# Cached attention: four score units in a row, then one whole value product; a VectorE read-out moved ahead of a transpose

## What is computed

```python
L = NPP * PSIZE                                   # 16 pages x 32 keys
kc = k_cache[block_table].reshape(bsz, L, HK, D)
k_all = jnp.concatenate([kc, k], axis=1)          # 512 cached keys + 32 own = 544
scores = jnp.einsum('bqhd,bkhd->bhqk', q, k_all) * SCALE
scores = jnp.where(valid[:, None, None, :], scores, -1e+30)
probs = jax.nn.softmax(scores, axis=-1)
o = jnp.einsum('bhqk,bkhd->bqhd', probs, v_all)
```

## Time and profile before

| | before |
|---|---|
| median of three runs | 3048.9 us |
| lowest, highest run | 3042.11, 3051.08 us |
| span of the profiled execution | 3042.6 us |
| TensorE matmul busy | 3015.9 us (99%) |
| VectorE busy | 1866.3 us (61%) |
| ScalarE busy | 1541.9 us (51%) |
| GpSimd busy | 609.8 us (20%) |

### The profile page before, as it was taken

One profiled execution on the slowest core, in us unless ns is written; L12 is line 12 of the kernel. 1 busy time (PEld: TensorE's weight loads), 2 busy tenths in 40 slices (PEclk: granted clock), 3 DMA queues, 4 the chain that ended last, 5 costly groups with the idle time before them and its releaser, 6 DMA issues.

```text
span 3042.6 us, 91714 instructions
## 1 busy us (share of the span) xinstructions
PE 3015.9 (99%) x36256; PEld 2345.8 (77%) x36256; DVE 1866.3 (61%) x3587; ACT 1541.9 (51%) x2949; POOL 609.8 (20%) x1462
## 2 busy tenths in 40 slices
PE   8999999899999999999999999999999999999999
PEld 7777778667777777777777888888888888888887
DVE  5777779487888888788786444432333333544544
ACT  6666655377777777777776222212333334322221
POOL 0000001354554554554551000000000000300000
PEclk9999999999999999999999999999999999999999
DMA  5333335566766666666667434413333333843311
GB/s 163 110 104 111 110 111 154 177 211 213 217 206 209 216 211 207 214 212 211 214 213 226 124 110 124 118 77 107 97 94 104 119 103 88 242 149 111 110 42 56
DMA packets 506613, 456.02 MB, mean 150 GB/s; under 512 B 33985, under 2 KB 470593, under 8 KB 501698
## 3 DMA queue, kind: packets, MB, share of 16 engines
q1 hardware_dynamic: 470402, 354.41, 38.4%
q0 software_dynamic: 35904, 96.85, 9.6%
HBM read 321.03 MB, written 130.02 MB: 148 GB/s over the span
## 4 chain that ended last, share of the span: by engine, by line
PE 79%; DMA 1%; DVE 0%; issue 0%; ACT 0%; DVEq 0%; SPq 0%
PE ps_o L1009 18%; PE ps_scores L993 16%; PE s_ps L58 8%; PE s_ps L60 8%; PE s_ps L59 8%; PE s_ps_proj L58 5%; PE s_ps_proj L59 5%; PE s_ps_proj L60 5%; PE s_ps_o L1542 1%; PE s_ps_scores L1518 1%; PE yv_ps L59 1%; PE yv_ps L60 1%; PE yv_ps L58 1%; PE s_ps L1717 0%; PE s_ps L1708 0%
## 5 line engine op out<-in xcount | busy, mean ns | idle before, releaser
L1009 PEld LDWEIGHTS ps_o<-weights_t,v_all 32*128 32x128 f32 x17408 | 510.2, 187 | 108.7 <-issue 108.6
L1009 PE MATMUL ps_o<-weights_t,v_all 32*128 32x128 f32 x17408 | 559.2, 276 | 4.1 <-issue 2.3
L993 PE MATMUL ps_scores<-k_slot,q_slot 128*32 128x288 f32 (+1 forms) x8192 | 525.7, 397 | 6.7 <-PEq L98 4.8
L898 ACT ACTIVATE probs<-masked,shift 128x544 f32<-128x544 f32 x512 | 382.9, 748 | 246.2 <-DVE shift L944 244.2
L944 DVE CUSTOM_DVE_ANT_0 masked<-ps_scores,reach,scale_now 128x544 f32<-128x544 f32 x512 | 390.1, 762 | 173.1 <-PE ps_scores L993 169.4
L993 PEld LDWEIGHTS ps_scores<-k_slot,q_slot 128*32 128x32 f32 x8192 | 242.1, 110 | 199.7 <-issue 8.6
L957 DVE STREAM_TRANSPOSE weights_t<-probs 128x544 f32<-128x544 f32 x512 | 376.8, 736 | 23.8 <-ACT probs L903 10.1
L903 ACT ACTIVATE probs<-probs,inv 128x544 f32<-128x544 f32 x512 | 375.7, 734 | 0.0
L1101 ACT ACTIVATE s_h_hi<-s_h_raw 128x2048 fp32r<-128x2048 f32 x64 | 122.8, 1919 | 487.4 <-PE s_ps L60 481.1
L84 POOL COPY k_slot<-k_pool 128x256 f32 x1024 | 358.9, 409 | 20.7 <-issue 20.1
L58 PE MATMUL s_ps_proj<-y_hi,s_w_hi 128*128 128x512 f32 x640 | 253.3, 396 | 0.0
(11 more groups left out here) (202 smaller groups left out, 4733.4 us busy)
## 6 DMA issues: line engine op xcount, KB each, us to landing
v_all<-vpool_in SPq DMA_DIRECT2D x1024, 128.0 KB, 3.0
qT_scratch<-k_pool SPq DMA_DIRECT2D x32, 1024.0 KB, 5.1
q_slot<-qT_scratch POOLq DMA_DIRECT2D x64, 512.0 KB, 3.5
oT_scratch<-o_t POOLq DMA_DIRECT2D x128, 256.0 KB, 4.9
s_h_raw<-oT_scratch SPq DMA_DIRECT2D x32, 1024.0 KB, 5.7
aT_scratch<-s_o_t SPq DMA_DIRECT2D x32, 1024.0 KB, 5.6
s_h_raw<-aT_scratch SPq DMA_DIRECT2D x32, 1024.0 KB, 5.7
w_raw<-w_in SPq DMA_DIRECT2D x11, 1024.0 KB, 7.7
```

The source lines that it names most:

```text
L898: act.activation(probs[:, k % BUF, :], masked[:, k % 2, :], ACT.Exp, bias=shift[:, k % BUF:k % BUF + 1], scale=-1.0, accum_out=total[:, k ...
L993: m = pe.matmul(ps_scores[q * S:(q + 1) * S, k % 2, cols], q_slots[j][:, head, r * S:(r + 1) * S], k_slots[j][:, pages, head * PSIZE:(head ...
L1009: m = pe.matmul(ps_o[:, q, 0:GS], v_all[rows, j, t, e * D:(e + 1) * D], weights_t[rows, g, :, t * S:(t + 1) * S], start=t == 0, stop=t == NPP)
```

## The change

TensorE now takes four units of scores in a row and then all 17 blocks of one group's values. On VectorE the second unit's `lowest` in each group is issued before the transpose that it used to follow; `inverse` stays between the two `lowest`. `reach_of` moves from the third unit of a batch to its fifth (`k % HK == G`), the first of its second group.

```diff
             def pair_of(i, first, last):
                 for k in range(2 * HK):
                     n, g = i * 2 * HK + k, k // G
-                    if k % HK == 2 and not (last and k > HK):
+                    if k % HK == G and not (last and k > HK):
                         reach_of(i * 2 + k // HK + 1, 1 - k // HK)
-                    lowest(n, k, i * 2 + k // HK)
+                    if k % G != 1:
+                        lowest(n, k, i * 2 + k // HK)
                     if not (first and k == 0):
                         inverse(n - 1, k - 1)
+                    if k % G == 0:
+                        lowest(n + 1, k + 1, i * 2 + k // HK)
                     if not (first and k < 2):
                         turn(n - 2, (k - 2) % (2 * HK), i * 4 + (k - 2) // G)
...
-            parts = (range(0, SPLIT), range(SPLIT, NPP + 1))
-
-            def pair_of(i, first):
-                for k in range(0, 2 * HK, 2):
-                    n, g = i * 2 * HK + k, k // G
-                    for d in range(2):
-                        scores(n + d, k + d, i * 2 + k // HK)
-                    if not (first and g < 2):
-                        values(i * 4 + g - 2, (g - 2) % 4, i if g >= 2 else i - 1, parts[k // 2 % 2])
...
+            for grp in range(GROUPS):
+                for n in range(grp * G, grp * G + G):
+                    scores(n, n % (2 * HK), n // HK)
+                if grp >= 2:
+                    values(grp - 2)
+            for grp in (GROUPS - 2, GROUPS - 1):
+                values(grp)
```

More of the change, by code:

```diff
@@ L987, in scores @@
                     pe.wait_ge(k_gathered, b + 1)
-                if not isinstance(n, int) or n >= 2:
+                if n >= 2:
                     pe.wait_ge(shift_done, n - 1)
@@ L995, in scores, with values @@
                 m.then_inc(scores_done, 1)
[L997 to L1006, removed]
+            def values(grp):
+                b, e, g = grp // 2, grp % 2, grp % 4
+                j = b % 2
+                if e == 0:
+                    pe.wait_ge(v_loaded[j], b // 2 * 16 * NPP + 16 * NPP)
+                    pe.wait_ge(v_own_loaded[j], b // 2 * 16 + 16)
+                pe.wait_ge(turned_w, grp * G + G)
+                pe.wait_ge(o_copied, grp + 1)
+                for t in range(NPP + 1):
                     for q in range(SEQ):
@@ L1010, in values @@
                                       weights_t[rows, g, :, t * S:(t + 1) * S], start=t == 0, stop=t == NPP)
-                if pages[-1] == NPP:
-                    m.then_inc(pv_done, 1)
-            parts = (range(0, SPLIT), range(SPLIT, NPP + 1))
-            def pair_of(i, first):
-                for k in range(0, 2 * HK, 2):
-                    n, g = i * 2 * HK + k, k // G
-                    for d in range(2):
-                        scores(n + d, k + d, i * 2 + k // HK)
-                    if not (first and g < 2):
-                        values(i * 4 + g - 2, (g - 2) % 4, i if g >= 2 else i - 1, parts[k // 2 % 2])
[L1024 to L1028, removed]
+                m.then_inc(pv_done, 1)
+            for grp in range(GROUPS):
[5 more added lines that the diff above has]
+                values(grp)
     return dict(sync=sync, gpsimd=gpsimd, scalar=scalar, vector=vector, tensor=tensor,
```

## The result

The changed kernel takes 3057.85 us (median of five runs, 3055.61 to 3060.11) against 3042.45 us before in the same rounds. The ratio on record is 1.0037, 95% interval 1.0025 to 1.0049: 0.37% slower, 11.3 us on 3042.45, with 7.6 to 14.9 inside the interval. It isn't the quotient of the two medians: these lie 15.4 us apart and the means 12.2, because the five runs before fall apart into three at 3042 and two at 3049 and 3051 us. The forecast was +10.3 us, 1.0034 times before.

What follows compares the result with a forecast made beforehand. TensorE was taken as the bound, busy 99% of the span. Per group 0.34 us saved against stalls of 0.40 and restart of 0.02 gave +10.0 us, the ends +0.3; on 3048.9 that made 3059.2 us, range 3049 to 3075.

Steps and rivals of the forecast that it cites:

- The fixed cost per change: TensorE's bursts: each pair of changes between scores and values costs 0.13 + 0.21 us; one pair less per group saves 43 us.
- The stall of the third unit: Scores burst: with two slots, the third unit waits for VectorE's lowest(0), starting at 2.22 or 2.30 us; stall 0.36 or 0.44.
- The first rival: Scores burst: the third unit does not stall, so the gain of 0.34 us per group stays, about 3006 us; chance 0.06.
- the third: Rival: the stall is only 0.36 us in all groups, or a few rare breaks vanish; +5, 3054 us; chance 0.09.
- The fourth unit at no cost: Scores burst: lowest(1) frees its slot by 3.14 us, before the third unit ends at 3.16; price 0, bounds 0 to 0.07.
- The group: Attention stage: a new group takes 8.20 us, 8.28 in a batch's first, against 8.16 before; 10.0 us over 125 groups.
- The mask: VectorE: reach_of at its new place does not meet GpSimd's copies, takes about 0.5 + 0.2 us and is priced 0.
- The second rival: VectorE: the mask meets GpSimd's copies and delays lowest(0), +22, 3082 us; with a held-up fourth unit (3073 us), chance 0.11.
- VectorE's and ScalarE's slack: Behind the burst: VectorE is done at 7.8 us, wanted at 9.6, 1.8 to spare; ScalarE's copy_o waits for values, free.
- The ends: First two groups, on VectorE's pace: one more unit is met at that pace, +0.3 us; the last values wait as before.
- The total: Whole kernel: 10.0 + 0.3 = +10.3 us, 3052.9 against the span of 3042.6, likeliest median 3059.2.

Runs made afterwards that it cites:

- e9: e8 with the small minimum of the two halves made a reduction over one two-element operand: 0.9879 times before, 3007.35 us.
- e4: The kernel before with a group's values cut into quarters, one unit of scores ahead of each, so four bursts of each kind per group: 1.0466 times before.
- e3: The changed kernel with lowest reading only 272 of the 544 columns (output not the reference's): 0.9922 times before.
- e1: TensorE's new order with VectorE's old one, against the kernel before: 1.0232 times before, 3115.62 us.
- e5: The changed kernel with the next batch's mask made at the end of a batch's last unit, beside GpSimd's gather: 3058.57 us in one run.
- e10: The changed kernel measured again, nothing altered: 1.0041 times before.
- e8: The changed kernel with the first two units' read-outs in halves, the first begun after 8 records; first two groups keep whole read-outs: 0.9962 times before.

## Why the prediction was right, point by point

- **The fixed cost per change** (0.13 + 0.21 us, 43 us in all) was right. e9, with the stall gone, has groups of 7.82 us, and e4's bursts have the same fixed parts. The runs show the cost, not what it is made of.
- **The stall of the third unit** was the step on which everything hung. Forecast 0.36 and 0.44 us, third unit at 2.22 and 2.30; the profile shows 2.22 and 2.30. e3 shows that it follows the length of the read-out. The first rival, that it would not come, fell with the chain of waits, and the third, 0.36 in all groups, with the burst medians of 4.19 and 4.27.
- **The fourth unit at no cost** was right, though with 0.02 us to spare. Its weight load waits for `shift` (idle 0.27) and comes at 3.14, and the burst goes on at the pace of an undisturbed one. In the other group the two units take 2.06 instead of 2.04: a price of 0.01 to 0.02, where I had kept 0 to 0.07. e1 shows what the moved `lowest` prevents.
- **The group**: 8.20 and 8.29 us against 8.20 and 8.28. Of 125 groups that makes the 10 us.
- **The mask** at its new place takes 0.445 us, forecast 0.5, and is hidden. The second rival did not come; in e5, with the mask beside the copies, its price did not come either. (Its 3082 and 3073 us are each 0.8 more than 3059.2 + 22 and + 13.)
- **VectorE's and ScalarE's slack** was as worked out: `copy_o` waits for the end of the values (112.7 us of idle time on ScalarE in the steady part) at no cost. VectorE was ready sooner than 7.8: its last transpose began 6.7 us into the group.
- **The ends** were put at +0.3 us. From the first scores to the start of unit 12 the stage took 22.1 us against 21.2 before: 0.9, of which 0.3 is one of the breaks. In e10 it took 21.3.
- **The total.** The profiled execution grew by 16.0 us, not 10.3; it is the slowest of the five runs. 5.2 of the 16.0 are the breaks without a releaser, which the prediction had at nothing. The groups' 10 us and the 0.6 at the start make 10.6; the ratio of all runs gives 11.3, with an interval that would also hold 8 or 14.
- **Luck in the absolute number.** 3059.2 lies 1.4 us from the measured 3057.85, but it was built on a median before of 3048.9; with two more runs that median fell to 3042.45. The difference of the medians, 15.4 us, is 5 over the forecast. What was foreseen well is the group, and the ratio bears it out.

## What to carry to other kernels

When work of one kind is put together to save the changes between two kinds, count the slots that the longer burst needs. With two slots, the third unit waits for start latency plus the whole read-out (1.37 + 0.79 + 0.06 us here) less two units' time, and that alone can return the gain. A slot needn't be freed whole: reading and releasing it in halves, the first half begun early (e8) and its small minimum kept out of GpSimd's way (e9), took the stall away and turned a loss of 0.4% into a gain of 1.2%. A third slot was not tried.

## What the runs showed of the hardware

- A VectorE operation on two 128x1 operands in SBUF took 122 ns at its median but up to 1131 ns beside GpSimd's copies; a reduction over one 128x2 operand at the same place took 105 to 153 ns, beside the copies or not. The Trainium skill, SBUF — State Buffer, "SBUF: two separate sides", says that a VectorE operation with two SBUF inputs shares a port pair, under an exclusive lock, with a GpSimd operation that reads SBUF. The two kernels agree with it: in e8 the slow records ended only with the last copy.
- The 128x512 mask took 1168 to 1687 ns in 41 of the 63 gathers before, until all the copies left were done, and 522 to 671 ns in the other 22, where one copy took 0.60 us instead. In e5 it took 534 ns at most. The same distance from the first copy, 4.14 us, gave both; the runs don't show what decides.
- After a stall within scores TensorE started at the pace of a burst's start: the fourth unit's weight load came 0.92 us after the third unit's start.
